# Graph network on one core: 50, 54 and 57 dense blocks in the three aggregations instead of 54 in each, seven of them built during the second and third

## The chip, the cores and the metric

One core of a Trainium2 chip, one launch. The metric is device time in microseconds (us), the median of the runs. Lower is better.

## What is computed

12,500 nodes with 128 features, and 400,000 edges sorted by their target `dst`, denser at low targets. The reference, cut:

```
h = relu(layernorm(x))
norm = deg_inv[src] * deg_inv[dst]
m = norm[:, None] * (h[src] + h[src] * h[dst] @ W1.T + b1)
x = x + leaky(segment_sum(m, dst))
h = relu(layernorm(x))
h = relu(h @ Ws0.T + (segment_sum(h[src], dst) / deg) @ Wn0.T + c0)
h =      h @ Ws1.T + (segment_sum(h[src], dst) / deg) @ Wn1.T + c1
x = x + h
```

There are three aggregations, each a segment sum of table rows over the edges of every target. The linear maps of the second and third are applied to the table before the sum.

## The kernel before, in words

The nodes are 98 tiles of 128 targets. An aggregation (`nth` = 0, 1, 2) computes each tile in one of two ways.

**Dense tiles**, the first `GROUPS` = 54 (most edges). Tile g has a count matrix ("block") of 128 targets by 12,544 sources in bf16, 3,136 KB, in one of two buffers `stage[0..1]`. The tile's sum is 98 matmuls (`product`, L1358), each with a block of 128 x 128 counts as weights and 384 columns (388 in aggregation 0) of the table `Xp`, which lies in SBUF in three bf16 parts.

**Tail tiles**, the other 44, are summed from gathered rows: one indirect DMA of 128 table rows for each 128 edges ("chunk") on GpSimd's queue (`gather`, L1187), a one-hot S on VectorE for each subgroup of up to five chunks (`ready`, L1601), and one matmul for each chunk (`subgroup`, L1296). A tail has 24 chunks at tile 54, 18 near the end and 12 in the last, 888 in all. The ring has room for five subgroups. `gather` and `ready` of a subgroup wait until the one five before has been used.

**Building a block** is done once, in aggregation 0. Edges of a node (or of two neighbours, from tile 14 on) are a "visit": a matmul (L1402) of a one-hot of the source's low 7 bits and a one-hot of its tile (128 x 196 with two nodes), into PSUM. From tile 16 on a block has 64 visits. VectorE makes one-hots for six visits at a time into one of three buffers (`one_hots`, L1573 and L1576), each buffer waiting until the visits that used it are done. ScalarE copies two visits' result out of PSUM into `stage` (`evict`, L1004); visits may be two such units ahead of it. SyncE stores the finished block to DRAM (L938). Step s of aggregation 0 runs the products of block s among the visits of block s+1, with at most one tail tile in it (44 tails over steps 2 to 53).

**Aggregations 1 and 2** build nothing. Two blocks are still in `stage`; for each step s from 2 on, SyncE loads one (`load_c`, L855: it waits for the end of step s-2). TensorE runs 98 products in each step, with the tail subgroups put among them at even distances (`due_at`). Each has 54 steps.

After its sum a tile goes through small work in a pipeline of places, two places for a step (dense, tail): `take`, `settle`, `finish`, `split_tile` on VectorE (L1648 to L1712), transposes and small fp32 matmuls on TensorE (L1308, L1316, L1324, L1334), copies on ScalarE (L1015, L1016, L1038 to L1070). In aggregation 2 only `take` is left. All queues are in program order, written out by hand.

**Ahead of aggregation 0** (0 to about 390 us) the edges are prepared: VectorE counts edges below each node, seven tiles at a time (L1473, L1474); after eight of these groups (`SPLIT_AT = 8 * HALF`, L1491) SyncE stores the first part of the edge positions and issues one small read for each of 36 batches of blocks (L841), later the second part (L844).

The order on TensorE in aggregations 1 and 2:

```
for i, (s, e) in enumerate(sequence):
    for j in drain_after[nth - 1].get(i, []): ...
    while n < n_subs and due_at[n] <= i:
        subgroup(nth, n)
        n += 1
    product(nth, s, e)
```

Of the kernel before, what the change touches and what calls it, by code (L numbers as in the profile page):

```python
# [16 lines left out]
P = 128  # L18
# [6 lines left out]
HALF = 7  # L25
# [7 lines left out]
GROUPS = 54  # L33
HEAD = GROUPS * P
TAIL_EDGE = 294400
# [32 lines left out]
def plan_batches(n_nodes, n_edges):  # L68
# [14 lines left out]
    for n in reversed(ns):  # L83
        vs = [visits_of(a, n, n_nodes, n_edges)]
        for count in ((8, 28, 32, 60) if a == 0 else (P // 2, P // 2) if vs[0] * P > 384 else (P,)):
            batches.append((a, n, [visits_of(a + i * n, n, n_nodes, n_edges) for i in range(count)]))
            a += count * n
    return batches
# [39 lines left out]
def program(nc, x, src, dst, W1, b1, Ws0, Wn0, c0, Ws1, Wn1, c1, out, n_nodes):  # L128
# [24 lines left out]
    units_of = [[q for q in range(len(units)) if unit_groups[q][0] == g] for g in range(GROUPS)]  # L153
    evicts_of = [max(evicts_to[q] - (len(unit_groups[q]) - 1 - unit_groups[q].index(g)) for q in range(len(units)) if g in unit_groups[q])
                 for g in range(GROUPS)]
    first_of = [min(q for q in range(len(units)) if g in unit_groups[q]) for g in range(GROUPS)]
# [3 lines left out]
    visits_in = [sum(unit_visits[q] for q in units_of[g]) for g in range(GROUPS)]  # L160
# [4 lines left out]
    assert hots_to[-1] == all_visits and all(r == 1 for r in rounds)  # L165

# [9 lines left out]
    n_subs = len(subs)  # L176
    gathered_to, so_far = [], [0] * RSUBS
    for u in range(3 * n_subs):
        so_far[u % RSUBS] += subs[u % n_subs][2]
        gathered_to.append(so_far[u % RSUBS])  # L180
    before_sub = [sum(n * max(1.0, 18 / tail_visits[i]) for i, _, n in subs[:u]) for u in range(n_subs)]
    due_at = [int(FIRST_DUE + (GROUPS * tiles - 8 - FIRST_DUE) * before_sub[u] / before_sub[-1]) for u in range(n_subs)]
    tail_at = [None] * GROUPS
    for i in range(tails):
        s = due_at[subs_of[i][-1]] // tiles
        assert s >= 2 and tail_at[s] is None
        tail_at[s] = i
    dense_at = [list(range(GROUPS))]
    for nth in range(1, 3):
        dense_at.append(dense_at[-1][:-3:-1] + dense_at[-1][:-2])  # L190
    places = 2 * GROUPS + EMPTY
    rank_at, order = [], []
    for nth in range(3):
        tile_at = [t for s in range(GROUPS) for t in (dense_at[nth][s], None if tail_at[s] is None else GROUPS + tail_at[s])]
# [3 lines left out]
    assert rows == tiles * P and tiles == loops * 2 * HALF and n_edges == iters * STEP and iters <= P and AT_ONCE * tiles <= BANK  # L198
# [9 lines left out]
    counts = nc.dram_tensor("counts", [GROUPS, P, tiles * P], BF16).ap()  # L208
# [6 lines left out]
    with ExitStack() as ctx:  # L215
# [85 lines left out]
        landing += [view(A_LAND, deepest[k] * P, 2) for k in range(2, n_batches)]  # L301
# [46 lines left out]
        SPLIT_AT = 8 * HALF  # L348
# [111 lines left out]
        def at(nth, p):  # L460

            return rank_at[nth][p] if 0 <= p < places else None

        def ticks_of(s):

            return range(2 * s, 2 * s + 2 if s < GROUPS - 1 else places)
# [19 lines left out]
        def during(w):  # L486

            return min(hot_at(w + 1) - 1 + HOTS, len(hots) - 1)
# [8 lines left out]
        for g in range(1, GROUPS):  # L497
            s = g - 1
            due = [] if tail_at[s] is None else subs_of[tail_at[s]]
# [5 lines left out]
            for e in range(2):  # L505
# [3 lines left out]
        last_due = [] if tail_at[GROUPS - 1] is None else subs_of[tail_at[GROUPS - 1]]  # L509
        hots_before_batch = [next(i for i in range(len(hots)) if hots[i][0] == k) for k in range(n_batches)]  # L510
        key_before = {hots_before_batch[k] + min(5, sum(f[0] == k for f in hots) - 1): k + 1 for k in range(1, n_batches - 1)}
        hot_of = [(i, e) for i, (_, m, _, _, n) in enumerate([(f[0], f[2], 0, 0, f[4]) for f in hots]) for e in range(m * n)]
        CAST, TURN_DST, GET_DST, TURN_SRC, GET_SRC = 100, 180, 230, 260, 310
        turned = (11, 11, deepest_tail - 22)
        assert GET_SRC < visits_in[0] - 20 and tails * 11 <= BANK and 0 < turned[2] <= 11
# [5 lines left out]
        sequence += [(1, e) for e in range(early // 2, tiles)] + [(s, e) for s in range(2, GROUPS) for e in range(tiles)]  # L521
        drain_after = ({10: [places], 18: [places + 1], 26: [places + 2], 50: [places + 3, places + 4, places + 5], 58: [places + 6], 66: [places + 7]},
                       {18: [places, places + 1, places + 2], 26: [places + 3], 34: [places + 4]})
        last_ticks = dict(zip((8, 28, 48, 62, 76, 82, 87, 91, 94, 96, 97), ticks_of(GROUPS - 1)))
        ready_after = [[] for _ in range(GROUPS)]
        for n in range(RSUBS, n_subs):
            ready_after[max(1, due_at[n - RSUBS] // tiles)].append(n)
        assert len(last_ticks) == EMPTY + 2 and at(1, 3) is None and at(2, 3) is None
# [284 lines left out]
        def _(sp):  # L813
# [89 lines left out]
            def load_ahead(nth, e):  # L903
# [6 lines left out]
                else:  # L910
                    sp.wait_ge(s_agg, nth * GROUPS)
# [3 lines left out]
            def last_step(nth):  # L915

                for j in ticks_of(GROUPS - 1):
                    load_next(nth, j)
# [5 lines left out]
            with sp.If(load_flag(sp, 0)):  # L924
# [7 lines left out]
                for g in range(GROUPS):  # L932
                    if g:
                        for j in ticks_of(g - 1):
# [7 lines left out]
                for nth in range(1, 3):  # L942
                    for k in range(3):
                        sp.wait_ge(s_pst[k], stored(k, nth * tiles))
                    if nth == 2:
                        for k in range(3):
                            sp.wait_ge(s_x1st[k], 16 * thirds(tiles, k))
                    load_first(nth)
                    for s in range(GROUPS - 1):
                        for j in ticks_of(s):  # L950
# [848 lines left out]
```

## Time and profile before

| | |
|---|---|
| median of 3 runs | 5116.73 us (5094.92 to 5118.95) |
| the profiled execution | 5090.41 us, span 5088.7 us |
| busy: TensorE / VectorE / ScalarE / GpSimd | 79% / 39% / 22% / 55% of the span |
| mean granted TensorE clock | 0.933 of 2.4 GHz |
| chain that ended last | TensorE 73%, of it L1358 53%, L1296 9%, L1402 7%; "issue" 11%; VectorE 7% |
| DMA | 914.9 MB, mean 180 GB/s |

Busy time of TensorE is that of modelled, overlapping matmuls, so it doesn't say how near the engine is to its limit. Starts of instructions and their distances are measured.

### The profile page before, as it was taken

To read this page: it belongs to the slowest core of one execution; us is meant where nothing else is said; L and a number is where in the kernel's file an instruction comes from. 1 tells how busy PE (TensorE), PEld (TensorE's weight loads), DVE (VectorE), ACT (ScalarE), POOL (GpSimd) and SP (SyncE) were. 2 spreads that over 40 slices of the span, in tenths; PEclk is the share of its full clock that TensorE was granted. 3 is DMA by queue.
4 is the path that set the end of the run, shared out by engine and by line. 5 is a ranking of instruction groups with operands and counts; after the bars stand their busy time and mean duration, and the time that the engine had idled before them with its cause. 6 is when DMAs were issued, how large, how long until landed. Compare 5 with 4: busy or idle time off the path is not lost.

```text
span 5088.7 us, 66517 instructions
## 1 busy us (share of the span) xinstructions
PE 3996.0 (79%) x24579; PEld 2352.5 (46%) x24579; DVE 1981.0 (39%) x5188; ACT 1129.7 (22%) x2916; POOL 2806.9 (55%) x2876
## 2 busy tenths in 40 slices
PE   0049677788788878888788888888888888888888
PEld 0035444455454545555444444544444444444444
DVE  3499566666565656565121122221211111111111
ACT  0034344455454545454000000000000000000000
POOL 5303533554645454552666666666646666666665
PEclk9999888899998999999899999999989999999999
DMA  4153334444444444456555555665665565566654
GB/s 140 36 137 125 116 129 143 144 164 165 154 161 146 167 149 164 152 169 215 203 209 209 211 211 209 218 222 205 225 224 206 208 217 212 197 226 213 212 209 170
DMA packets 384983, 914.86 MB, mean 180 GB/s; under 512 B 74278, under 2 KB 318543, under 8 KB 363929
## 3 DMA queue, kind: packets, MB, share of 16 engines
q1 hardware_dynamic: 193728, 603.15, 31.9%
q0 software_dynamic: 132960, 275.90, 18.3%
q10 hardware_dynamic: 57968, 31.48, 2.3%
q8 instruction: 202, 3.31, 0.3%
q14 instruction: 125, 1.02, 0.1%
HBM read 672.23 MB, written 238.88 MB: 179 GB/s over the span
## 4 chain that ended last, share of the span: by engine, by line
PE 73%; issue 11%; DVE 7%; another core or an unknown queue 4%; ACT 2%; DMA 2%; SPq 0%; POOL 0%; ACTq 0%; DVEq 0%; POOLq 0%
PE ps L1358 53%; PE ps L1296 9%; PE ps L1402 7%; ACT arena L1004 2%; PE ps L1324 2%; DVE arena L1573 2%; DVE arena L1576 2%; DMA arena<-in_src 1%; DMA table<-arena 1%; PE ps L1316 0%; PE ps L1308 0%; DVE stats L1479 0%; SPq L816 0%; DVE arena L1474 0%
## 5 line engine op out<-in xcount | busy, mean ns | idle before, releaser
L1187 POOL DMA_INDIRECT arena<-parts,arena x2664 | 2643.3, 992 | 1732.5 <-issue 718.1
L1358 PE MATMUL ps<-arena 128*128 128x384 bf16 (+1 forms) x15876 | 3296.7, 340 | 366.5 <-issue 321.9
L1358 PEld LDWEIGHTS ps<-arena 128*128 128x128 bf16 x15876 | 1566.2, 101 | 1458.1 <-issue 642.0
L1402 PE MATMUL ps<-arena 128*128 128x196 bf16 (+1 forms) x4910 | 1018.5, 245 | 421.1 <-issue 166.1
L1004 ACT ACTIVATE arena<-ps 128x392 bf16<-128x392 f32 x1728 | 848.5, 498 | 1088.1 <-PE ps L1402 832.1
L1601 DVE TENSOR_TENSOR arena<-arena 128x640 bf16<-128x640 bf16 (+1 forms) x582 | 268.9, 464 | 1866.5 <-remote 1485.9
L1402 PEld LDWEIGHTS ps<-arena 128*128 128x128 bf16 x4910 | 459.2, 103 | 730.6 <-issue 277.2
L1573 DVE TENSOR_TENSOR arena<-arena 128x768 bf16<-128x768 bf16 (+3 forms) x848 | 457.2, 539 | 667.0 <-PE ps L1402 513.9
L1296 PE MATMUL ps<-arena 128*128 128x384 bf16 (+1 forms) x2664 | 571.2, 340 | 53.0 <-issue 48.7
L1576 DVE TENSOR_TENSOR arena<-arena 128x1176 bf16<-128x1176 bf16 (+4 forms) x848 | 528.2, 623 | 0.0
L1296 PEld LDWEIGHTS ps<-arena 128*128 128x128 bf16 x2664 | 266.3, 101 | 270.6 <-issue 115.3
L1062 ACT ACTIVATE arena<-ps 128x128 f32<-128x128 f32 x196 | 54.3, 277 | 1018.3 <-remote 742.6
L1648 DVE TENSOR_REDUCE arena<-ps 128x128 f32<-128x384 f32 x294 | 163.0, 554 | 262.5 <-remote 177.8
L1177 POOL DMA_INDIRECT arena<-records,first_edge x36 | 48.0, 1334 | 335.6 <-PE ps L1266 321.0
L1324 PE MATMUL ps<-w_t,arena 128*128 128x256 f32 x392 | 125.0, 400 | 12.9 <-issue 7.4
L1152 POOL DMA_INDIRECT arena<-in_dst,arena x98 | 97.0, 990 | 54.8 <-issue 29.5
L1015 ACT ACTIVATE arena<-ps 128x128 bf16<-128x128 f32 x196 | 54.0, 275 | 215.9 <-remote 66.9
L1247 PE MATMUL ps<-ident,arena 128*56 128x128 f32 x1 | 0.4, 416 | 103.2 <-DVE arena L1491 103.2
L1016 ACT ACTIVATE arena<-ps 128x256 f32<-128x256 f32 x196 | 75.5, 385 | 0.1
L1324 PEld LDWEIGHTS ps<-w_t,arena 128*128 128x128 f32 x392 | 63.6, 200 | 21.7 <-issue 18.8
L1709 DVE TENSOR_TENSOR arena<-arena,bias 128x128 f32<-128x128 f32 x196 | 56.1, 286 | 28.6 <-ACT arena L1016 28.3
L1712 DVE TENSOR_TENSOR arena<-arena 128x128 bf16<-128x128 f32 x196 | 57.4, 293 | 6.7
(155 smaller groups left out, 1180.1 us busy)
## 6 DMA issues: line engine op xcount, KB each, us to landing
arena<-counts SPq DMA_DIRECT2D x104, 3136.0 KB
counts<-arena SPq DMA_DIRECT2D x54, 3136.0 KB
arena<-parts,arena POOLq DMA_INDIRECT x2664
arena<-parts SPq DMA_DIRECT2D x28, 672.0 KB, 9.6
arena<-table SPq DMA_DIRECT2D x196, 64.0 KB
parts<-arena ACTq DMA_DIRECT2D x110, 96.0 KB
parts<-arena SPq DMA_DIRECT2D x14, 679.0 KB, 6.9
parts<-arena SPq DMA_DIRECT2D x86, 96.0 KB
```

The source lines that it names most:

```text
L1004: act.activation(stage[g % 2][:, :, f - g * P:t - g * P], ps[:, q % 2, (f - a) * tiles:(t - a) * tiles].rearrange("p (n a) -> p a n", n=t ...
L1016: act.activation(yS[:, n % 3, :], bank(7, 0, 2 * P), ACT.Copy).then_inc(s_yS, 1)
L1152: pool.indirect_dma_start(near[q % 7][:, t % HALF, :], None, dst.rearrange("(c e) -> c e", e=P), bass.IndirectOffsetOnAxis(ap=near_i[:, t: ...
L1187: pool.indirect_dma_start(ring[:, m % RSUBS * CHUNKS + c, 0:W0 if nth == 0 else W1C], None, parts_of[nth], bass.IndirectOffsetOnAxis(ap=ta ...
L1296: t = pe.matmul(bank(b, 0, w), S[:, e, :], ring[:, e, 0:w], start=first + c == 0, stop=first + c == tail_visits[i] - 1, skip_group_check=True)
L1324: pe.matmul(bank(7, 0, 2 * P), hT[:, r % 2, :], w_t[:, 2 * nth + 1:2 * nth + 3, :].rearrange("p k f -> p (k f)"), start=True, stop=True).t ...
L1358: m = pe.matmul(bank(b, 0, w), stage[k][:, a, :], Xp[:, a, 0:w], start=e == 0, stop=e == tiles - 1, skip_group_check=True)
L1402: pe.matmul(bank(q % 2, b * n * tiles, (b + 1) * n * tiles), hot_low[f % HOTS][:, c * P:(c + 1) * P], hot_key[f % HOTS][:, c * n * tiles:( ...
L1573: dve.tensor_tensor(hot_low[f % HOTS][:, 0:visits * P].rearrange("p (v f e) -> p v f e", v=visits, e=2), low[:, k % 2, at_c, :].unsqueeze( ...
L1576: dve.tensor_tensor(hot_key[f % HOTS][:, 0:visits * width].rearrange("p (v f e) -> p v f e", v=visits, e=2), key[:, k % 2, at_c, :].unsque ...
L1601: dve.tensor_tensor(S[:, e:e + count, :].rearrange("p c (f e) -> p c f e", e=2), tail_rel[:, i, first:first + count, :].unsqueeze(2).to_br ...
L1648: then(dve.tensor_reduce(agg, bank(b, 0, PARTS * P).rearrange("p (k f) -> p f k", k=PARTS), AX.X, ALU.add))
```

## The change

Aggregation nth has `STEPS[nth]` dense blocks: 50, 54, 57, and 48, 44, 41 tails (984, 888, 818 chunks). Aggregation 0 builds blocks 0 to 49. In aggregation 0 every step from 2 to 49 has one tail. During steps 11, 22, 33 and 44 of aggregation 1, blocks 50 to 53 are built for the next step, and stored after it; aggregation 2 builds blocks 54 to 56 during steps 13, 27 and 41 (64 visits each, 448 in the seven). In such a step the visits stand among products 20 to 93, use PSUM banks 4 and 5, and are copied out into the buffer of step s+1, for which nothing is loaded. The one-hots come on VectorE after the step's two ticks and before `ready`; the copies on ScalarE are cut in two by the second tick. The records of these blocks are landed at the start of the aggregation (two more indirect DMAs on GpSimd's queue), turned in steps 2 and 4. `SPLIT_AT` is 9 groups, the batches are 38, and the tail edges kept start at 283,264 instead of 294,400.

```diff
-GROUPS = 54
+STEPS = (50, 54, 57)
+GROUPS = STEPS[0]
-TAIL_EDGE = 294400
+TAIL_EDGE = 283264
...
-        SPLIT_AT = 8 * HALF
+        SPLIT_AT = 9 * HALF
...
+    built_in = [{}, dict(zip((12, 23, 34, 45), range(STEPS[0], STEPS[1]))), dict(zip((14, 28, 42), range(STEPS[1], STEPS[2])))]
...
+        ends_at = {due_at[nth][subs_of[i][-1]] // tiles if nth else i + steps - tails_of[0]: i for i in range(steps - GROUPS, tails_of[0])}
...
             def load_c(nth, s):
                 k = stage_of(nth, s)
-                sp.wait_ge(s_agg, nth * GROUPS + s - 1)
+                sp.wait_ge(s_agg, steps_before[nth] + s - 1)
+                if s - 2 in built_in[nth] and nth == 1:
+                    sp.wait_ge(s_counts[k], 16 * stores_to[built_in[nth][s - 2]])
...
-                        if s + 2 < GROUPS:
+                        if s + 2 < STEPS[nth] and s + 2 not in built_in[nth]:
                             load_c(nth, s + 2)
+                        if s + 1 in built_in[nth] and nth == 1:
+                            g, k = built_in[nth][s + 1], stage_of(nth, s + 1)
+                            sp.wait_ge(s_evict, evicts_of[g])
+                            sp.dma_start(counts[g], stage[k].rearrange("p a n -> p (a n)")).then_inc(s_counts[k], 16)
...
+                        for i, j in enumerate(ticks_of(nth, s)):
+                            if nth == 1:
+                                tick(nth, j)
+                            for q in here[15 * i:15 + 17 * i]:
+                                if q == here[0]:
+                                    act.wait_ge(s_agg, steps_before[nth] + s)
+                                evict(q, k, 4)
...
+            def visit(w, bank_0):
+                q, c_0, j, v = visit_at[w]
+                width = batches[units[q][0]][1] * tiles
+                if w == visits_to[q] - unit_visits[q] and q >= 2:
+                    pe.wait_ge(s_evict, evicts_to[q - 2])
+                f, c = hot_of[w]
+                if c == 0:
+                    pe.wait_ge(s_hot, f + 1)
+                pe.matmul(bank(bank_0 + q % 2, c_0, c_0 + width), ...).then_inc(s_visit, 1)
...
                         product(nth, s, e)
+                        if s + 1 in built_in[nth]:
+                            g = built_in[nth][s + 1]
+                            if e == 20:
+                                pe.wait_ge(s_key, batches_to[nth])
+                                pe.wait_ge(s_w1free, tiles)
+                            for w in range(starts_at[g], starts_at[g + 1]):
+                                if 20 + (w - starts_at[g]) * 75 // visits_in[g] == e:
+                                    visit(w, 4)
...
+                        if s + 1 in built_in[nth]:
+                            g = built_in[nth][s + 1]
+                            for f in range(hot_at(starts_at[g]), hot_at(starts_at[g + 1])):
+                                one_hots(f)
+                        for n in ready_after[nth][s]:
                             ready(nth, n)
```

## Rows read from the trace of the kernel before

**Rows 1.** Each engine by stage; stretches cut at block stores and loads.

```profile
core 0: us, PE busy (x) PEld busy (x) DVE busy (x) ACT busy (x) POOL busy (x), PEclk, DMA share, GB/s
1075.20:2359.70 1284.50, 1053.12 (x6891) 658.89 (x6891) 780.10 (x2040) 646.52 (x1574) 663.11 (x633) 0.94 0.47 159
2359.70:2417.50 57.80, 51.11 (x295) 30.86 (x296) 27.40 (x111) 13.52 (x49) 4.08 (x5) 0.97 0.86 276
2417.50:3703.10 1285.60, 1103.01 (x6090) 616.37 (x6089) 252.48 (x719) 93.59 (x360) 839.81 (x872) 0.95 0.60 211
3791.30:5039.10 1247.80, 1066.13 (x5788) 580.09 (x5788) 195.88 (x463) 0.00 (x0) 819.91 (x851) 0.91 0.60 214
```

**Rows 2.** Waits (engine, line, releaser: us, times, longest), aggregation 2.

```profile
DVE arena L1601 <- remote: 712.5, 106, 13.8
PEld ps L1358 <- issue: 289.6, 618, 3.2
POOL arena L1187 <- issue: 232.3, 758, 0.8
POOL arena L1187 <- remote: 186.1, 83, 4.7
```

**Rows 3.** TensorE's timeline in aggregation 1, one step's part.

```profile
2928.01 3.90 PE L1358 MATMUL ps<-arena 128*128 128x384 bf16 x23
2931.75 0.81 PE L1296 MATMUL ps<-arena 128*128 128x384 bf16 x4
...
2933.86 0.27 PE L1316 MATMUL ps<-ident,arena 128*128 128x128 f32 x1
2933.97 0.60 PE L1324 MATMUL ps<-w_t,arena 128*128 128x256 f32 x2
2934.41 2.01 PE L1358 MATMUL ps<-arena 128*128 128x384 bf16 x10
...
2937.52 0.32 PE L1358 MATMUL ps<-arena 128*128 128x384 bf16 x1 [0.39 <-issue]
2938.25 0.32 PE L1358 MATMUL ps<-arena 128*128 128x384 bf16 x1 [0.41 <-issue]
```

**Rows 4.** The block stores around the four steps without a tail, SyncE's timeline.

```profile
1219.86 0.32 SPq L938 DMA_DIRECT2D counts<-arena  x1
1251.06 0.32 SPq L938 DMA_DIRECT2D counts<-arena  x1
...
1408.64 0.32 SPq L938 DMA_DIRECT2D counts<-arena  x1
1434.81 0.32 SPq L938 DMA_DIRECT2D counts<-arena  x1
...
1659.63 0.32 SPq L938 DMA_DIRECT2D counts<-arena  x1
1691.20 0.32 SPq L938 DMA_DIRECT2D counts<-arena  x1
...
1945.15 0.32 SPq L938 DMA_DIRECT2D counts<-arena  x1
1974.79 0.32 SPq L938 DMA_DIRECT2D counts<-arena  x1
```

**Rows 5.** Groups by form, 1075.2 to 2359.7: ScalarE's copies, VectorE's one-hots, GpSimd's gathers.

```profile
L1004 ACT ACTIVATE arena<-ps 128x392 bf16<-128x392 f32 x1153 | 564.7, 499 | 637.9 <-PE ps L1402 508.1 <-remote 88.6 <-issue 35.6
L1576 DVE TENSOR_TENSOR arena<-arena 128x1176 bf16<-128x1176 bf16 x377 | 288.4, 765 | 0.0
L1573 DVE TENSOR_TENSOR arena<-arena 128x768 bf16<-128x768 bf16 x376 | 208.0, 553 | 447.7 <-PE ps L1402 382.3 <-remote 60.4 <-issue 4.0
L1187 POOL DMA_INDIRECT arena<-parts,arena x617 | 647.4, 1049 | 587.8 <-PE ps L1296 405.1 <-issue 159.0 <-remote 23.7
```

**Rows 6.** Waits in the same stretch of aggregation 0.

```profile
PEld ps L1402 <- issue: 168.1, 221, 4.3
PEld ps L1402 <- ACT arena L1004: 147.6, 149, 3.4
```

**Rows 7.** Preparation: SyncE's timeline, then VectorE's.

```profile
180.32 20.79 SPq L841 DMA_DIRECT2D arena<-ends_d  x36
212.31 0.33 SPq L844 DMA_DIRECT2D ends_d<-arena  x1
...
176.26 0.22 DVE L1491 SCALAR_TENSOR_TENSOR arena<-arena 128x56 f32<-128x56 f32 x1 [9.22 <-issue]
189.59 1.09 DVE L1473 TENSOR_TENSOR arena<-arena 128x896 bf16<-128x896 int32 x1
```

**Rows 8.** VectorE's timeline in aggregation 1: first and last row around a step's two ticks.

```profile
2926.85 0.55 DVE L1648 TENSOR_REDUCE arena<-ps 128x128 f32<-128x384 f32 x1
...
2931.19 0.43 DVE L1601 TENSOR_TENSOR arena<-arena 128x512 bf16<-128x512 bf16 x1
```

More of the change, by code:

```diff
@@ L87, in plan_batches @@
             a += count * n
+    for first, last in zip(STEPS, STEPS[1:]):
+        for g in range(first, last, 2):
+            batches.append((g * P, 2, [visits_of(g * P + i * 2, 2, n_nodes, n_edges) for i in range(P if g + 1 < last else P // 2)]))
     return batches
@@ L159, in program @@
     assert all(len(unit_groups[q]) == 1 and unit_groups[q][0] < CHECKED_TO for q in checked)
-    visits_in = [sum(unit_visits[q] for q in units_of[g]) for g in range(GROUPS)]
+    visits_in = [sum(unit_visits[q] for q in units_of[g]) for g in range(STEPS[2])]
     starts_at = [int(a) for a in np.cumsum([0] + visits_in)]
@@ L165, in program @@
     assert hots_to[-1] == all_visits and all(r == 1 for r in rounds)
+    batches_to = [sum(b[0] < n * P for b in batches) for n in STEPS]
+    hots_in = [sum(batches[f[0]][0] < n * P for f in hots) for n in STEPS]
+    assert all(batches[f[0]][1] == 2 for f in hots[hots_in[0]:])
     tails = tiles - GROUPS
@@ L176, in program @@
     n_subs = len(subs)
-    gathered_to, so_far = [], [0] * RSUBS
[L178 to L192, printed above, removed]
-    for nth in range(3):
-        tile_at = [t for s in range(GROUPS) for t in (dense_at[nth][s], None if tail_at[s] is None else GROUPS + tail_at[s])]
+    tails_of = [tiles - n for n in STEPS]
+    first_sub = [subs_of[STEPS[nth] - GROUPS][0] for nth in range(3)]
+    steps_before = [sum(STEPS[:nth]) for nth in range(4)]
@@ new lines, in program @@
+    due_at, tail_at, dense_at, order, rank_at, places = [], [], [], [], [], []
+    for nth in range(3):
+        steps = STEPS[nth]
+        before_sub = [sum(n * max(1.0, 18 / tail_visits[i]) for i, _, n in subs[first_sub[nth]:u]) for u in range(n_subs)]
+        due_at.append([int(FIRST_DUE + (steps * tiles - 8 - FIRST_DUE) * before_sub[u] / before_sub[-1]) for u in range(n_subs)])
+        ends_at = {due_at[nth][subs_of[i][-1]] // tiles if nth else i + steps - tails_of[0]: i for i in range(steps - GROUPS, tails_of[0])}
+        assert len(ends_at) == tails_of[nth] and min(ends_at) >= 2
+        tail_at.append([ends_at.get(s) for s in range(steps)])
+        if nth == 0:
+            dense_at.append(list(range(steps)))
+        else:
+            kept = iter(dense_at[-1][:-3:-1] + dense_at[-1][:-2])
+            dense_at.append([built_in[nth][s] if s in built_in[nth] else next(kept) for s in range(steps)])
+        places.append(2 * steps + EMPTY)
+        tile_at = [t for s in range(steps) for t in (dense_at[nth][s], None if tail_at[nth][s] is None else GROUPS + tail_at[nth][s])]
@@ L197, in program @@
         rank_at.append([None if t is None else order[nth].index(t) for t in tile_at])
-    assert rows == tiles * P and tiles == loops * 2 * HALF and n_edges == iters * STEP and iters <= P and AT_ONCE * tiles <= BANK
+    loads_to, stores_to, so_far = {}, {}, [[0, 0], [GROUPS // 2, GROUPS // 2]]
+    for nth in range(1, 3):
+        for s in range(2, STEPS[nth]):
+            k = (s + nth) % 2
+            if s in built_in[nth]:
+                so_far[1][k] += nth == 1
+                stores_to[built_in[nth][s]] = so_far[1][k]
+            else:
+                so_far[0][k] += 1
+                loads_to[nth, s] = so_far[0][k]
     assert all(len(o) == tiles for o in order) and (n_edges - TAIL_EDGE) % P == 0
@@ L300, in program @@
         landing = [view(A_X, deepest[0] * P, 2), view(A_X + 2 * P * deepest[0], deepest[1] * P, 2)]
-        landing += [view(A_LAND, deepest[k] * P, 2) for k in range(2, n_batches)]
+        landing += [view(A_LAND + (2 * P if k > batches_to[0] and (k - batches_to[0]) % 2 else 0), deepest[k] * P, 2) for k in range(2, n_batches)]
         assert 2 * P * max(deepest[2:]) <= 1280 and 2 * P * (deepest[0] + deepest[1]) <= XP_COLS
@@ L460, in at, with ticks_of @@
         def at(nth, p):
-            return rank_at[nth][p] if 0 <= p < places else None
-        def ticks_of(s):
-            return range(2 * s, 2 * s + 2 if s < GROUPS - 1 else places)
+            return rank_at[nth][p] if 0 <= p < places[nth] else None
+        def ticks_of(nth, s):
+            return range(2 * s, 2 * s + 2 if s < STEPS[nth] - 1 else places[nth])
         def stage_of(nth, s):
@@ L498, in program @@
             s = g - 1
-            due = [] if tail_at[s] is None else subs_of[tail_at[s]]
+            due = [] if tail_at[0][s] is None else subs_of[tail_at[0][s]]
             for e, n in enumerate(due):
@@ L1729, in _ @@
                 dve.wait_ge(s_iotak, 1)
-                for f in range(len(hots)):
+                for f in range(hots_in[0]):
                     if f in key_before:
```

200 lines of the change are left out of this document (114 added, 86 removed).

## Prediction

> **What bounds the kernel now.** I read the page's chain of waits first: TensorE holds 73% of it. Then the engines by stage [rows 1], cut at the stores and loads of blocks so that each stretch is whole steps. Aggregation 0 from block 18 on is 36 steps in 1284.5 us, 35.7 each. Aggregation 1 is 51 steps in 1285.6 us, 25.2 each; aggregation 2 is 51 in 1247.8 us, 24.5 each. The reader is to see that in aggregations 1 and 2 VectorE and ScalarE are nearly empty (252 and 94 us of 1286, then 196 and none), GpSimd is busy two thirds and DMA 60%. The waits [rows 2] settle between TensorE and GpSimd: GpSimd, apart from 0.3 us ahead of each gather, stands 186 us waiting for ring room, that is for TensorE to use an old subgroup, while TensorE has no wait for a gather among its large ones, only "issue". So TensorE's stream is the bound in both, with room on GpSimd of some 15%.
>
> TensorE's stream [rows 3]: 23 products start within 3.74 us, 0.163 each, at full clock; then come stretches where one starts every 0.7 us with nothing named that it waits for. Over the whole of aggregation 2, 51 x 98 products and some 51/54 of 888 gather matmuls are 5837 in 1247.8 us, 0.214 each. The difference to 0.163 is the granted clock (0.91, so 0.179) and those stalls. So a matmul of 384 columns costs between 0.179 (if stalls are not caused by it) and 0.214 us (if they are). I take 0.214, since the stalls are spread through the whole stretch (618 of them on L1358's weight loads [rows 2]).
>
> In aggregation 0 the step holds visits too. Four steps in the stretch have no tail; the distances of the stores around them are 31.2, 26.2, 31.6 and 29.6 us [rows 4], mean 29.6. The other 32 take (1284.5 - 118.6) / 32 = 36.4. So there a tail costs 6.8 us, against 20 x 0.214 = 4.3 for its matmuls alone. Of 29.6, 98 products are 98 x 0.214 x 388/384 = 21.2 and a tile's small work about 1 (in aggregation 1 it is 0.55, from 2933.86 to 2934.41 [rows 3], and aggregation 0 has two more products). What is left, 7.4 us, is the price of a block's 64 visits, with the waits that they bring. By columns alone they are 64 x 196/384 x 0.163 = 5.3. ScalarE's copies of two visits are 0.499 us and the one-hots for six visits 0.553 + 0.765 = 1.32 [rows 5]; TensorE's waits in front of visits are half "issue", half ScalarE's copy [rows 6].
>
> A rule bears on these stalls. The Trainium skill ("Runtime: NRT & Kernel Launch", Instruction fetch mechanics) says that the sequencer fetches its instructions in 16 KiB blocks by its own DMA queue, and that this is mostly hidden. By that rule no stall belongs to an instruction as such, a visit costs its columns alone, and the sum below is 7 x 2.1 = 15 us smaller; the stalls of 0.7 us in the trace are then something else, and no row tells what.
>
> **Aggregation 0: four blocks fewer, four tails more.** Four steps go: products, visits, copies, one-hots, stores. Without their tails they are 4 x 29.6 = 118.6 us. 48 tails instead of 44, and the four new ones have 24 chunks, not 20: 4 x (6.8 + 4 x 0.214) = 30.6. Small work of 98 tiles stays. Sum **-88**. Bounds: dearest and cheapest tail-less step, and a tail at its matmuls alone (24 x 0.214 = 5.1) or at 7.7: -4 x 31.6 + 20.5 = -106, to -4 x 26.2 + 30.6 = -74. GpSimd: a gather is 1.05 us and 0.3 ahead of it [rows 5], so 24 chunks are 32 us in the early steps, and later 20 are 27, both inside a step of 36 us; it waited 405 us for ring room in this stretch, so I cost its extra 96 gathers at nothing. If that cover were gone, they would be 96 x 1.35 = 130 us.
>
> **Aggregation 1: four blocks built.** Each 7.4 us of visits. Added to that: in the step that builds, the one-hots stand behind VectorE's two ticks, which take 4.3 us [rows 8], then 1.3 for the first; TensorE reaches product 20 after some 20 x 0.163 + 0.8 of a tail's matmuls + 0.5 of small work = 4.6 us, so it waits about 1 us. The last visit is at product 93, and the next step's first product waits for its copy: 0.5 us and the way there, against four products (0.65). About 1 us more. Behind the waiting visits on TensorE stand only products of the same step; behind one-hots on VectorE stand `ready` of subgroups due more than a step later. So 4 x (7.4 + 2) = **+38**. Records turned and keys made in steps 2 and 4: two small transposes each, under 1 us together. DMA: the build takes away a load (3,136 KB) in one step and puts load and store together in the next. A step moves 25.2 us x 211 GB/s = 5.3 MB; with a store 8.5 MB; at the most that a stretch shows (276 GB/s at a share of 0.86 [rows 1], so 321 if full) that is 26.6 us, over the step's 25.2. The load stands ahead of the store on SyncE's queue, and the tile reads behind it are three places early, so I take nothing; as a bound, 3.5 us each. Bounds: visits by columns alone 4 x 5.3 = +21; with everything 4 x 13 = +52.
>
> **Aggregation 2: three more steps, 70 chunks fewer, three blocks built.** 294 x 0.214 = +62.9; -70 x 0.214 = -15.0; 3 x (7.4 + 1), since VectorE's ticks are shorter there and ScalarE is idle, +25.2. Loads are 52 as before. Sum **+73**. Bounds: matmuls at 0.179 and visits at 5.3, 52.6 - 12.5 + 16 = +56; to 62.9 - 12.5 + 3 x 10 = +80.
>
> **Preparation.** VectorE gives the first edge positions one group of seven tiles later, 189.6 instead of 176.3 us, 13.3 later [rows 7]. SyncE's small reads (36 in 20.8 us, 0.578 each) then start at 193.6 and 38 of them end at 215.6; the second store, at 212.3 now, goes behind them. **+3.3**; nothing hides it, since the last part's reads are what VectorE waits for next.
>
> **Sum.** -88 + 38 + 73 + 3 = **+26** on the profiled execution's 5090.4 us, so 5117. That execution lies 26 below the median of the runs shown (5116.7), inside their spread; on the median it is **5143 us**. In words: aggregation 0 gives back four blocks, but the kernel builds three more in all, and at its bound engine products moved from the first to the last aggregation cost the same. TensorE's columns alone: 98 products fewer (-392 + 294), 26 gather matmuls more (+96 - 70), 192 visits more.
>
> **Rivals.**
>
> *The visits cost only their columns*, since they fill the 0.7 us stalls: -88 + 21 + (48 + 16) + 3 = 0, or +11 with the waits at both ends of a build; time 5117 to 5128. For it: nearly idle VectorE and ScalarE, and no load in a building step. Against: aggregation 0, where the same mix costs 7.4.
>
> *Faster: visits and waits vanish in idle time.* If steps of aggregation 0 are set by the round trip visit, copy, next visit, the four steps are worth the bound of -106, and in aggregations 1 and 2 the same visits run in the time in which TensorE now starts nothing (about 5 us a step). Then -106 + 8 + 51 + 3 = -44, or with -88 for the steps -26: 5073 to 5091, the middle 5082. It decides from below 3 us a block, not 7.4. For it: ScalarE's copy ends 148 us of waits in front of visits [rows 6], 4 us a step. The Trainium skill ("Perfetto Trace Analysis", Identifying the Most-Contended Engine) judges TensorE's headroom by weight-load busy share; here that is 616 of 1286 us, 48%, which would leave room for them. Against: TensorE's order is written by hand, a visit waits in line, and GpSimd waits for it.
>
> *Slower by more: the building steps stall.* If the first one-hot comes after S and ticks that themselves wait, or load and store collide, 5 to 6 us for each of seven steps on top: about +61, 5178. For it: VectorE waits long in `ready` (712 us in 106 times, 6.7 each [rows 2]), and what follows it in order is late by as much. Against: those waits end with TensorE's own progress.
>
> **How the numbers follow.** The change could be told from none beyond 0.5%, 26 us, here. Forecast 0.45, visits by columns 0.20, faster rival 0.17, large stalls 0.18. The forecast's own range is 5127 to 5165, half of it beyond 26 us. With the other cases: 5095 to 5185. Faster 0.15 (most of its rival), same 0.38 (the second case and the lower half of the forecast, with the faster rival's edge), slower 0.47.
>
> **What would show it.** Block stores: the last of the 50 near 2270 to 2275 instead of 2359.7, steps with a tail still 36. Loads of aggregation 1: ordinary distances 25 us, building steps 34 to 35. Aggregation 2: ordinary 24.5 and building 33. GpSimd's wait for ring room in aggregation 0 down by half but not gone; TensorE with no waits on gathers. Wrong if aggregation 0's steps grow past 37 (gathers late), if a building step takes under 29 us, or over 38, or if the granted clock of a stage moves by more than 0.02, which is 25 us in a stage and in no term of mine.

## The result and the profile after

| | before | after |
|---|---|---|
| median | 5117.84 us (4 runs, 5094.92 to 5136.64) | 4987.82 us (4 runs, 4966.84 to 5001.77) |
| ratio | | 0.974, 95% interval 0.969 to 0.980 |
| the profiled execution | 5090.41 us, span 5088.7 | 4966.84 us, span 4965.1 |
| mean granted clock | 0.933 | 0.946 |

Faster by 2.6%, where 0.5% slower was forecast and the widest range began at 5095 us. By stage, cut at the first block store, the first load of aggregation 1 and the first of aggregation 2:

| us | preparation | aggregation 0 | aggregation 1 | aggregation 2 |
|---|---|---|---|---|
| before | 390.8 | 2026.7 | 1373.8 | 1297.3 |
| after | 395.1 | 1942.4 | 1398.1 | 1229.4 |
| difference | +4 | -84 | +24 | **-68** |
| predicted | +3 | -88 | +38 | **+73** |

All of the surprise is in aggregation 2. It does three more dense steps and builds three blocks, and takes 68 us less.

The engines by stage (the stretches of the second and third row hold nearly the whole of aggregations 1 and 2); they answer to [rows 1]:

```profile
core 0: us, PE busy (x) PEld busy (x) DVE busy (x) ACT busy (x) POOL busy (x), PEclk, DMA share, GB/s
950.00:2180.00 1230.00, 999.44 (x6538) 626.69 (x6536) 755.36 (x1990) 601.93 (x1484) 717.69 (x689) 0.94 0.50 163
2330.00:3720.00 1390.00, 1208.33 (x6798) 687.20 (x6795) 324.98 (x874) 164.74 (x522) 874.39 (x904) 0.94 0.60 209
3740.00:4960.00 1220.00, 1093.79 (x6420) 625.60 (x6417) 233.85 (x538) 47.53 (x98) 765.73 (x792) 0.97 0.61 216
```

TensorE starts 6420 matmuls in 1220 us of aggregation 2, one in 0.190 us; before it was one in 0.216 (5788 in 1247.8 us [rows 1]). The granted clock is 0.97 instead of 0.91. So the mean distance of two starts, which the prediction had taken for a price, is another one here. The waits of the changed kernel in aggregation 2, which answer to [rows 2] (L1434 is the product, L1242 the gather, L1681 `ready`):

```profile
engine line waited for: us in total, times, longest us
DVE arena L1681 <- remote: 524.2, 70, 12.4
POOL arena L1242 <- issue: 179.4, 587, 0.9
POOL arena L1242 <- remote: 144.7, 66, 2.9
PEld ps L1434 <- issue: 140.0, 263, 2.0
```

These are of 3850 to 4850. TensorE's unexplained "issue" gaps on the weight loads fall from 290 us in 618 pieces of 1248 us [rows 2] to 140 us in 263 pieces of 1000. GpSimd's waits at the head of a subgroup (L1242, "remote") stay: 145 us of 1000, where it was 186 of 1248.

The loads on SyncE's timeline around a building step of aggregation 1 and one of aggregation 2; a built block needs no load, so the distance there spans two steps (58.02 us from 2569.83, 54.66 from 3963.27):

```profile
2545.85 0.32 SPq L887 DMA_DIRECT2D arena<-counts  x1
2569.83 0.32 SPq L887 DMA_DIRECT2D arena<-counts  x1
2627.85 0.32 SPq L887 DMA_DIRECT2D arena<-counts  x1
2649.40 0.32 SPq L887 DMA_DIRECT2D arena<-counts  x1
...
3942.57 0.32 SPq L887 DMA_DIRECT2D arena<-counts  x1
3963.27 0.32 SPq L887 DMA_DIRECT2D arena<-counts  x1
4017.93 0.32 SPq L887 DMA_DIRECT2D arena<-counts  x1
4040.69 0.32 SPq L887 DMA_DIRECT2D arena<-counts  x1
```

In aggregation 1 the ordinary step is 24.4 us (median) and the four double distances are 58.0, 57.1, 62.9 and 56.7, so a built block costs some 9.9 us (58.7 - 48.8). In aggregation 2 the ordinary step is 22.1 (25.4 before), the three double ones 54.7, 52.7 and 53.6: 9.5 each.

### The profile page after: what moved, and what is told of

It reads as the page before. It is cut to its first block, busy times and chain, and to the rows that moved or that the text cites. A ratio compares the mean times of both kernels' runs of the same rounds, so it can differ in the third digit from the quotient of the medians.

```text
span 4965.1 us, 67044 instructions
## 1 busy us (share of the span) xinstructions
PE 3948.1 (80%) x24703; PEld 2352.8 (47%) x24703; DVE 2022.3 (41%) x5265; ACT 1174.3 (24%) x3014; POOL 2846.9 (57%) x2906
## 4 chain that ended last, share of the span: by engine, by line
PE 72%; issue 10%; DVE 7%; another core or an unknown queue 5%; ACT 3%; DMA 2%; SPq 0%; POOL 0%; ACTq 0%; DVEq 0%; POOLq 0%
PE ps L1434 51%; PE ps L1357 9%; PE ps L1407 8%; ACT arena L1038 2%; DVE arena L1653 2%; PE ps L1385 2%; DVE arena L1656 2%; DMA table<-arena 1%; DMA arena<-in_dst 1%; PE ps L1377 0%; PE ps L1369 0%; DVE stats L1559 0%; SPq L846 0%; DVE arena L1729 0%
## 5 line engine op out<-in xcount | busy, mean ns | idle before, releaser
L1242 POOL DMA_INDIRECT arena<-parts,arena x2690 | 2679.9, 996 | 1730.9 <-issue 716.3
L1434 PE MATMUL ps<-arena 128*128 128x384 bf16 (+1 forms) x15778 | 3245.8, 337 | 264.9 <-issue 224.6
L1434 PEld LDWEIGHTS ps<-arena 128*128 128x128 bf16 x15778 | 1550.4, 100 | 1295.5 <-issue 465.8
L1407 PE MATMUL ps<-arena 128*128 128x196 bf16 (+1 forms) x5102 | 1076.2, 246 | 462.8 <-issue 189.0
L1038 ACT ACTIVATE arena<-ps 128x392 bf16<-128x392 f32 x1824 | 892.5, 498 | 1919.1 <-PE ps L1407 1469.6
L1681 DVE TENSOR_TENSOR arena<-arena 128x640 bf16<-128x640 bf16 (+1 forms) x587 | 269.4, 463 | 1591.7 <-remote 1286.3
L1653 DVE TENSOR_TENSOR arena<-arena 128x768 bf16<-128x768 bf16 (+3 forms) x881 | 475.9, 540 | 695.9 <-PE ps L1407 598.5
L1357 PE MATMUL ps<-arena 128*128 128x384 bf16 (+1 forms) x2690 | 573.6, 341 | 30.6 <-issue 21.3
L1656 DVE TENSOR_TENSOR arena<-arena 128x1176 bf16<-128x1176 bf16 (+4 forms) x881 | 553.5, 628 | 0.0
```

The source lines that it names most:

```text
L1038: act.activation(stage[k][:, :, a - g * P:b - g * P], ps[:, bank_0 + q % 2, 0:(b - a) * tiles].rearrange("p (n a) -> p a n", n=b - a), ACT ...
L1242: pool.indirect_dma_start(ring[:, m % RSUBS * CHUNKS + c, 0:W0 if nth == 0 else W1C], None, parts_of[nth], bass.IndirectOffsetOnAxis(ap=ta ...
L1357: t = pe.matmul(bank(b, 0, w), S[:, e, :], ring[:, e, 0:w], start=first + c == 0, stop=first + c == tail_visits[subs[n][0]] - 1, skip_grou ...
L1407: pe.matmul(bank(bank_0 + q % 2, c_0, c_0 + width), hot_low[f % HOTS][:, c * P:(c + 1) * P], hot_key[f % HOTS][:, c * width:(c + 1) * widt ...
L1434: m = pe.matmul(bank(b, 0, w), stage[k][:, a, :], Xp[:, a, 0:w], start=e == 0, stop=e == tiles - 1, skip_group_check=True)
L1653: dve.tensor_tensor(hot_low[f % HOTS][:, 0:visits * P].rearrange("p (v f e) -> p v f e", v=visits, e=2), low[:, k % 2, at_c, :].unsqueeze( ...
```

## The experiments

Theories. **Price**: the prediction's, each TensorE instruction costs what the mean shows, 0.214 us for 384 columns. **Pace**: aggregations 1 and 2 last as long as the gathers need, so a dense block more is nearly free and a gather less is worth about 1.4 us. **Chance**: the granted clock of the one profile moved. The stage of aggregation 2 is quoted for every kernel, since the kernels differ there. The runs went to different chips. The kernel before takes 5,098 and 5,100 us on one of them (two batches of runs), 5,049 on another, and 4,257 (one run) and 4,259 on two more; the first two chips and that of the first pair (5,118) are "the slower chips", the last two "the faster chips". Whole times are compared only with the kernel before on the same chip.

### The kernel before again, and the change in parts

The kernel before, and three kernels made of the change by its tuple and the steps that build: s50_54_54 builds nothing in aggregation 2; s54_54_57 builds nothing in aggregation 1 and has the 44 tails of aggregation 0 as before; s50_54_60 builds six blocks in aggregation 2, for steps 9, 18, 27, 36, 45 and 53.

```diff
-STEPS = (50, 54, 57)
+STEPS = (50, 54, 54)
+STEPS = (54, 54, 57)
+STEPS = (50, 54, 60)
```

> The kernel before once more, for a second profile of its stages. Chance theory (the last aggregation lay at a low clock, 0.91, in that one profile): its 52 loads span clearly less than the 1247.8 us of before, by 40 us or more. Both other theories (a matmul has a fixed price on TensorE; gathered chunks set the pace): 1248 us within 15.

> The change without its last part: aggregation 2 with 54 blocks, 888 chunks, nothing built in it. My prediction's prices: aggregation 0 gives 85 us, aggregation 1 costs 25, aggregation 2 as before, so 5057 where before is 5117. If the gain of the last aggregation comes from its 70 chunks fewer (chunk theory), the same number, and the whole change is 70 us faster than this one. If it comes from something else in the changed code, such as freer queues, this one is at 4990 already.

> The last part alone: 54 blocks in aggregations 0 and 1, three more built in aggregation 2 and 818 chunks in it. My prediction's prices: +73 there and +3 in the preparation, about 5193 against 5117. Chunk theory (time of aggregation 2 goes with its chunks, 1.46 us each): -68 +3, about 5052.

> Sixty blocks in aggregation 2, six built there, 760 chunks or so. My prediction's prices: another 73 us on top of the change. Chunk theory: another 58 chunks less at 1.46 us, minus nothing, so 50 to 85 us faster than the change, about 4920. A third theory, that TensorE and GpSimd are near each other: TensorE takes over between 57 and 60, so within 25 us of the change or slower.

Measured on one slower chip (kernel before 5097.81, median of 13 runs):

| | us | ratio, interval | aggregation 0 | 1 | 2 | gathers in 2 |
|---|---|---|---|---|---|---|
| again_54 | 5074.27 | | 2007.8 | 1366.3 | 1304.7 | 888 |
| s50_54_54 | 5056.18 | 0.992, 0.989 to 0.995 | 1990.3 | 1396.0 | 1299.4 | 888 |
| s54_54_57 | 5020.63 | 0.985, 0.980 to 0.990 | 2051.3 | 1373.4 | 1220.0 | 818 |
| s50_54_60 | 4924.61 | 0.967, 0.962 to 0.972 | 1963.3 | 1400.4 | 1161.8 | 749 |

Chance falls: two more traces with 888 gathers have 1299 and 1305 us. The gain belongs to the third number alone: with three more blocks there and nothing else, about -80 us; with six, about -140. Each block more is some -23 to -27 us, against +24 by price. Price falls. s50_54_60 beats both kernels, by 3.3% against the kernel before.

### What paces aggregation 2: gathers, matmuls or products left out

Five edits of the kernel before, each in aggregation 2 alone. (1) x_fewgather, r_fewgather (the count that TensorE waits for is lowered with it):

```diff
-                for c in range(count):
+                for c in range(count if nth < 2 else 1):
                     pool.indirect_dma_start(ring[...], None, parts_of[nth], ...)
```

(2) x_fewmm, r_fewmm: the same edit around the matmul of `subgroup`. (3) x_fewprod, r_fewprod:

```diff
-                m = pe.matmul(bank(b, 0, w), stage[k][:, a, :], ...)
+                if nth < 2 or e % 3 != 1 or e == tiles - 1:
+                    m = pe.matmul(bank(b, 0, w), stage[k][:, a, :], ...)
```

(4) x_narrow:

```diff
-ring[:, ..., 0:W0 if nth == 0 else W1C], None, parts_of[nth]
+ring[:, ..., 0:W0 if nth == 0 else W1C if nth == 1 else P], None,
+parts_of[nth] if nth < 2 else parts_of[nth].rearrange("r (k f) -> (r k) f", f=P)
```

(5) x_smallload, and r_narrow and r_smallload, which are (4) and (5) once more:

```diff
-                sp.dma_start(stage[k]..., counts[dense_at[nth][s]])
+                cols = tiles * P if nth < 2 else 4 * P
+                sp.dma_start(stage[k]...[:, 0:cols], counts[dense_at[nth][s], :, 0:cols])
```

> The kernel before, but in aggregation 2 each gathered row has 128 columns of bf16 and not 384 (the tail tiles' sums are not the reference's; instructions and their number are unchanged). If the gathers' traffic holds up TensorE, aggregation 2 falls from 1300 us to about 1160, as with 60 blocks. If it is GpSimd's issue, or TensorE's own price, it stays at 1300 within 15.

> The kernel before, but in aggregation 2 only the first chunk of each subgroup is gathered, 194 of 888 (tail sums not the reference's); TensorE's instructions are unchanged. My prediction's price (a matmul costs 0.214 us whatever is gathered): 1300 us. If gathering sets the pace in any way, traffic or GpSimd: about 54 x 18.6 + ends = 1040 to 1080.

> The kernel before, but in aggregation 2 only one matmul for each subgroup, 694 fewer (tail sums not the reference's); all 888 gathers stay. My prediction's price: 694 x 0.214 = 149 us less, 1150. If GpSimd's 1.27 us a chunk set the pace: unchanged, 1285 to 1300. Something of both gives a fall by 694 x 0.163 = 113 at most.

> The kernel before, but in aggregation 2 each block load brings 128 KB and not 3,136 (dense sums not the reference's). If block loads cause TensorE's stalls, aggregation 2 falls by up to 240 us. If gathering does, it stays within 20 us, since the gathers are as many as before.

> The kernel before once more, for its stages on the chip that the other kernels of this call run on. Two chips have been seen so far: one on which it takes about 5,100 us (aggregation 2: 1,305 us for 888 gathers, 1.47 us each) and one on which it took 4,256.5 us once, with no profile. If the pace of GpSimd's gathers sets aggregations 1 and 2 on the faster one: both near 888 x 1.27 = 1,130 us, with TensorE's idle time put down to the gathers' transfers. If TensorE's stream sets them there: no such waits, and TensorE busy to the end of every step.

> The kernel after, on the same chip. Gather pace: aggregation 2 shorter than in r_54 in proportion to its gathers, 818 of 888, so by 8%: about -90 us on a chip where it takes 1,120, -100 where it takes 1,300; aggregation 1 (888 in both) within 30 us. TensorE's stream at a fixed price for each instruction (the prediction's): aggregation 2 longer by 3 x 98 x 0.214 + 192 visits less 70 matmuls, +73 us, on either chip. Total by gather pace: -84 (aggregation 0) + 30 - 90 to 100 = about -140; by the fixed price +26.

> Leaves out, in aggregation 2 of the kernel before, all gathers of a subgroup but its first (194 instead of 888); the matmuls stay, on old rows of the ring. Gather pace: aggregation 2 falls by over 100 us, to what TensorE's stream alone takes. On a chip where it takes 1,300: if the gathers only hold TensorE back through its 'issue' gaps, these fall from some 240 us to under 100 and the stage to 1,060 to 1,150; if the gaps are TensorE's own (one for so many instructions), the stage stays within 30 us of 1,300. On a chip where it takes 1,120: about 995, as seen once.

> Leaves out, in aggregation 2 of the kernel before, all matmuls on gathered rows but one for each subgroup (194 instead of 888); all gathers stay. Gather pace: the stage changes by under 20 us (1,126 was seen once on the faster chip). Fixed price for each matmul: 694 x 0.214 = -149 us.

> Leaves out, in aggregation 2 of the kernel before, 32 of the 98 products of each step (1,728 of 5,292); all gathers, their matmuls, one-hots and block loads stay. What TensorE must do falls from about 990 us at the full clock (6,180 matmuls of 0.16) to about 715. A pace of the gathers that belongs to GpSimd and its transfers alone: the stage stays within 30 us of the 1,290 to 1,305 seen on the slower chip (of 1,123 on the faster). GpSimd alone at its 1.27 us an issue and nothing else slower: 1,130 on both chips, which would make the 170 us above it on the slower one a coupling of TensorE's work with the gathers. TensorE's fixed price: 1,728 x 0.214 = -370 us, to about 930.

> As x_fewprod (32 of 98 products left out in aggregation 2 of the kernel before; all gathers and their matmuls stay), in the hope of the slower chip. If the gathers have a pace of 1.46 us there whatever TensorE does, the stage stays at 1,290 to 1,305 us. If TensorE's own work slows them down, it falls to 1,130, GpSimd's issue alone. On a faster chip it repeats 1,123.

The stage of aggregation 2, in us:

| | gathers | matmuls on them | products | slower chips | faster chips |
|---|---|---|---|---|---|
| kernel before | 888 | 888 | 5,292 | 1304.0 (r_54) | no profile; its aggregation 1, with 888 too: 1153 to 1159 |
| few gathers | **194** | 888 | 5,292 | **995.7** | **995.5** |
| few gather matmuls | 888 | 194 | 5,292 | 1286.1 | 1126.4 |
| few products | 888 | 888 | 3,564 | 1280.4 | 1122.9 |
| narrow rows | 888 | 888 | 5,292 | | 1120.5 |
| small block loads | 888 | 888 | 5,292 | | 1123.3 |
| the change (r_57) | 818 | 818 | 5,586, and 192 visits | 1228.2 | |

Taking 694 matmuls or 1,728 products away from TensorE gives 18 and 24 us, where price has 149 and 370; taking gathers away gives 308 us on the slower chip and some 128 on the faster. With so few gathers TensorE alone needs 996 us on either chip. r_fewprod ran on another slower chip than the rest of its column (kernel before 5048.79 there, aggregation 1 1340 us against 1367 in r_54, which bounds how much of its 24 us is the chip's). On the faster chips the stage is 1,120 to 1,126 us in all four kernels with 888 gathers: the row widths and the loads don't matter. r_narrow and r_smallload were meant for a slower chip but ran on another faster one and gave 1124.5 and 1119.7. So it isn't shown for the slower chips that the bytes of gathers and loads don't matter there.

On the faster chip TensorE stands waiting for gathered rows, as here in x_fewprod:

```profile
3618.41 1.44 PE L1296 MATMUL ps<-arena 128*128 128x384 bf16 x4 [3.58 <-DMA arena<-parts,arena]
```

GpSimd's line between the first and the last load of the stage, in x_fewprod, r_54, r_57 and r_fewprod, in this order (busy, mean of one | idle before, by releaser):

```profile
L1187 POOL DMA_INDIRECT arena<-parts,arena x861 | 820.5, 953 | 262.3 <-issue 259.0 <-PE ps L1296 3.4
```

```profile
L1187 POOL DMA_INDIRECT arena<-parts,arena x854 | 824.1, 965 | 432.3 <-issue 237.2 <-remote 180.7 <-PE ps L1296 14.4
```

```profile
L1243 POOL DMA_INDIRECT arena<-parts,arena x788 | 766.1, 972 | 419.4 <-issue 212.0 <-remote 170.3 <-PE ps L1358 37.1
```

```profile
L1187 POOL DMA_INDIRECT arena<-parts,arena x869 | 833.3, 959 | 412.6 <-issue 250.2 <-remote 147.6 <-PE ps L1296 14.8
```

The reader is to see two terms. Busy and "issue" together are one price per gather in all four: 1079.5 / 861 = 1.25, 1061.3 / 854 = 1.24, 1.24 and 1.25 us. On the faster chip that is all, the engine never stops. On the slower ones a second term stands beside it, pauses at the head of a subgroup: 195 us (r_54), 207 (r_57) and 162 (r_fewprod). They shrink little when a third of the products goes. With 190 us taken for them, a fit and no more, aggregation 2 would be gathers x 1.24 + 190: 888 x 1.24 + 190 = 1291 (1297 to 1305 measured), 818: 1204 (1220 to 1229), 749: 1119 (1162). It is 16 to 25 us short at 57 blocks and 43 at 60, as TensorE's own stream comes nearer.

TensorE's waits over the same stretches, in r_54, r_fewgather and r_fewprod:

```profile
PEld ps L1358 <- issue: 295.8, 595, 4.1
```

```profile
PEld ps L1358 <- issue: 0.7, 1, 0.7
```

```profile
PEld ps L1359 <- issue: 455.7, 864, 2.7
```

The gaps are no property of TensorE's instructions: they vanish without the gathers and grow when products are left out. Nor are they the fetching of instructions: r_fewgather moves the same 46 blocks on the DMA queue for instructions as r_54. One such stretch in r_fewprod, TensorE, then GpSimd, then VectorE:

```profile
4206.62 2.76 PE L1359 MATMUL ps<-arena 128*128 128x384 bf16 x16
4209.22 0.81 PE L1296 MATMUL ps<-arena 128*128 128x384 bf16 x4
...
4213.64 0.32 PE L1359 MATMUL ps<-arena 128*128 128x384 bf16 x1 [1.08 <-issue]
...
4215.81 0.48 PE L1359 MATMUL ps<-arena 128*128 128x384 bf16 x1 [0.79 <-issue]
4216.51 0.48 PE L1296 MATMUL ps<-arena 128*128 128x384 bf16 x1 [0.22 <-issue]
4218.60 0.48 PE L1296 MATMUL ps<-arena 128*128 128x384 bf16 x1 [1.61 <-issue]
4220.01 0.49 PE L1296 MATMUL ps<-arena 128*128 128x384 bf16 x1 [0.94 <-issue]
4221.39 0.48 PE L1296 MATMUL ps<-arena 128*128 128x384 bf16 x1 [0.89 <-issue]
4221.67 4.39 PE L1359 MATMUL ps<-arena 128*128 128x384 bf16 x15
```

```profile
4217.27 0.95 POOL L1187 DMA_INDIRECT arena<-parts,arena  x1 [0.30 <-issue]
4218.52 0.95 POOL L1187 DMA_INDIRECT arena<-parts,arena  x1 [0.30 <-issue]
4221.75 1.01 POOL L1187 DMA_INDIRECT arena<-parts,arena  x1 [2.28 <-remote]
```

```profile
4221.52 0.82 DVE L1602 TENSOR_TENSOR arena<-arena 128x512 bf16<-128x512 bf16 x2 [3.82 <-remote]
```

Matmuls trickle, one in 0.7 to 2 us, and TensorE is quick again as GpSimd resumes (4221.67, 4221.75). Counting groups of two and more starts that are over 0.6 us apart, with at most 1 us of quick starts between them, r_fewprod has 51 in 1,245 us, mean 10.4 us, of which 50 hold a pause of GpSimd of over 0.6 us; r_54 has 55 of mean 5.7 and r_57 44 of mean 3.5, and every one holds a pause. In these three the median distance from a group's end to the nearest end of a pause is 0.4 us. x_fewprod, on the faster chip, has no such group and no pause.

The pause isn't the wait for TensorE that the program's text suggests. Gather and `ready` wait on one semaphore, which the last matmul of the subgroup five before raises. Here that is the last of the four from 4209.22 on, which started at 4209.71, and both waiting engines go on 12 us later, 0.23 us apart. So it is in the others: of 91 pauses in r_54, 86 began after the needed matmul had ended (its end is modelled, its start measured), and the gather came a median 6.9 us after that end, with some 20 further matmuls started; 55 of 55 in r_fewprod, with 12.4 us. Two controls: in r_fewgather, on r_54's chip, 186 of 187 pauses end 0.27 us after the needed matmul, and on a faster chip, in s50_56_60 below, all 107 do. So on the slower chips both engines learn late that a matmul is done, at the end of a stretch in which TensorE trickles. Whether the matmul ends later than its modelled end or the signal is late, and what holds up both, isn't shown; it goes with the gathers.

r_57 repeated the result on the slower chip: 4985.23 us, ratio 0.975 (0.970 to 0.980); its stages 1957.7, 1397.8 and 1228.2 against r_54's 2008.5, 1367.1 and 1304.0.

### Does it hold in aggregation 1, and on other chips

s50_56_60 has STEPS = (50, 56, 60), six blocks built in aggregation 1 (for steps 9, 18, 27, 36, 45 and 51) and four in aggregation 2 (for 11, 22, 33 and 45). r_57b is the changed kernel again.

> 50, 56 and 60 dense blocks, six built in aggregation 1 and four in aggregation 2: 841 or so gathers in aggregation 1 in place of 888, 750 in aggregation 2 as in the variant 50, 54, 60. Gather pace: aggregation 1 about -65 us for some 45 gathers less, +15 for two more built blocks and their waits, aggregation 2 about -15 (two blocks fewer to build): 4,925 - 65 = about 4,860 on the slower chip. Fixed price for TensorE's instructions: +45 us in aggregation 1, so about 4,950.

> The kernel after, beside r_fewprod. On the slower chip again 4,985. On a faster one, where aggregation 2 of the kernel before takes 1,123 us for 888 gathers: the gathers' pace gives 818 x 1.27 = 1,039, TensorE at the full clock 0.16 x (57 x 98 + 818) + 31 for the visits = 1,056; so about 1,065, with TensorE as the bound, and the whole kernel about 4,256 - 45 (aggregation 0) + 10 - 58 = 4,165. The prediction's fixed price would give more than 4,256.

r_57b came on the chip of r_fewprod: 4936.19 against 5048.79 us, ratio 0.976 (0.972 to 0.981), aggregation 2 1208.5. The gain is the same on the slower chips (0.974, 0.975, 0.976). s50_56_60 came on a faster chip: 4172.34 against 4259.06 us, ratio 0.980 (0.978 to 0.982), so neither of its numbers could be met as written. Its stages are 1560.0, 1146.7 and 1094.8, where kernels like the one before have 1596 to 1607 and 1153 to 1159 in aggregations 0 and 1, and in aggregation 2 about 1,130 (the edited kernels' 1,120 to 1,126, whose whole times are 7 to 15 us under the kernel before). The engines from the first to the last load of its aggregation 2, and then those of x_fewprod:

```profile
3074.90:4123.10 1048.20, 1046.61 (x6535) 630.73 (x6533) 235.37 (x528) 64.05 (x130) 717.93 (x738) 1.00 0.70 250
```

```profile
3126.80:4208.50 1081.70, 799.17 (x4198) 438.51 (x4197) 194.68 (x464) 0.00 (x0) 819.64 (x861) 0.86 0.70 247
```

With 60 blocks TensorE starts 6,535 matmuls in 1,048 us, one in 0.160, at the full clock (2.4 GHz), and GpSimd waits 141 us for it: the bound has moved from GpSimd to TensorE. So past about 60 blocks no more should be had on the faster chips; none was run with more. On the slower chips s50_54_60 is half way there: only 34 of its 95 pauses began after the needed matmul had ended. In aggregation 1 six built blocks and 47 gathers less gave about -8 us there, where the expectation for a slower chip had -50; there too TensorE is the bound now, busy 99% of the time (1062.75 of 1075 us from 1975 on, at clock 1.00). On a slower chip this kernel wasn't run, nor was the changed kernel on a faster one: whether 56 pays there, and what 57 gives here, is open.

## Why the prediction was wrong

**The preparation**, +3.3: +4.3 measured; right, though traces of one kernel differ here by up to 11 us.

**Aggregation 0**, -88: -84 in the first pair. Over all traces on slower chips but the one at 5,049 us (six with 54 blocks: mean 2023; four with 50: mean 1963) it is -60, less than the smaller bound of -74, and r_57 against r_54 is -51. The sign holds, the size was half as large again as what came, and the first pair's agreement was partly luck. Part of the miss is the term for the four added tails, 30.6 us: they fall in the first 18 blocks, whose stores take 45 us more in the first pair (684.5 to 729.1) and 44 in the second (680.6 to 724.2).

**Aggregation 1**, +38: +30 (means 1398 of four and 1368 of six traces). A building step costs 9.4 predicted and 9.9 by the loads' distances; what the pairs of stages lack, the ordinary steps give back (24.4 against 25.1).

**Aggregation 2**, +73: -68 in the first pair, -76 in the second and over the means (1301 and 1226). This is the step that failed, in these words: "So TensorE's stream is the bound in both, with room on GpSimd of some 15%", and from it "294 x 0.214 = +62.9; -70 x 0.214 = -15.0". The mean distance of TensorE's starts, 0.214 us, was taken as a price; it was the quotient of a stage set by the gathers and the number of matmuls in it. The runs put in its place: products next to nothing (1,728 fewer gave 24 us at most), 70 gathers x 1.24 = -87, and the three building steps, which do cost something locally (9.5 each by the loads) but leave the ordinary steps shorter. The 11 us between -87 and -76 are not put down to anything by a run. The "room" was misread from its rows: "stands 186 us waiting for ring room, that is for TensorE to use an old subgroup" holds for few of these waits. In the trace of the kernel before, 85 of the 91 pauses began after the needed matmul had ended, and the gather followed a median 6.6 us after that end. So they say nothing of TensorE's stream as the bound; they are a part of the gathers' pace on the slower chips and no reserve.

The prediction had the hint in its own rows: stalls of 0.7 us "with nothing named that it waits for" are nearly a quarter of the stage (290 of 1248 us [rows 2]), and it priced instructions by them. Its lower bound, 0.179, still made each block a cost; a bound of nothing, by the reading that TensorE had time over, was left out. GpSimd's extra gathers of aggregation 0 were costed at nothing, and the same question wasn't asked the other way round for the gathers that go.

**The rivals.** "Faster: visits and waits vanish in idle time" had the right sign and the right place in part (TensorE's idle time), but it still charged 51 us for aggregation 2, and 5082 is 94 us above the result. The Trainium skill ("Perfetto Trace Analysis", Identifying the Most-Contended Engine), which judges by weight-load busy share, was the better guide: 48% in aggregation 1 [rows 1], and products did fit in. Between the first and last load of aggregation 2 the share is 577.85 of 1255.20 us (46%) in r_54 and 60% in s50_56_60, where TensorE is at its limit. "The visits cost only their columns" and "slower by more" fell.

**What was to show it.** Blocks' last store in aggregation 0: 2278.8, near the 2270 to 2275 named, but 2301.7 in r_57. Building steps lie in the stated 29 to 38 us (33.6 and 31.6 by the double distances). Ordinary steps of aggregation 2 were to be 24.5 and are 22.1. The clock is the sign of a wrong sum that came: it was to move by at most 0.02 and moved by 0.06 in that stage.

## What to carry to other kernels

An engine that is "busy" and has unnamed small gaps all through a stage isn't shown to be the bound: look at what each other engine spends on one of its instructions too, and see what repeats (here about 1.24 us of GpSimd for a gather, on every chip). A wait on a semaphore isn't a wait for the work that raises it unless that work ends just before: compare the two times. Where GpSimd issues a gather for each 128 rows, count gathers first; here a matmul more cost next to nothing until TensorE's starts were 0.16 us apart without gaps. Kernels that leave out work, on either side, settled this, and a change should be tested on the size beside it: of those tried on a slower chip 60 was better than 57.

## What the runs showed of the hardware that was not expected

- The same kernel takes 5,100 us on one chip and 4,257 on another. The three aggregations are 13 to 20% shorter on the latter, the preparation 7% (about 395 and 368 us); aggregation 2 without most of its gathers takes 996 us on both.
- An indirect gather of 128 rows of 768 bytes costs GpSimd 1.25 us from start to start, and with 256-byte rows the stage is the same (1120.5 against 1123).
- On the slower chips VectorE and GpSimd go on a median 2 to 12 us after the modelled end of the matmul whose semaphore they wait for, both at once; on a faster one (s50_56_60) 0.27 us after it. The stage's time doesn't tell this, only the two times side by side do.
- The granted clock was higher where TensorE had less idle time. Between the first and last load of aggregation 2, on slower chips, its mean and TensorE's busy share were 0.78 and 71% (r_fewprod), 0.86 and 81% (r_fewmm), 0.92 and 85% (r_54), 0.97 and 90% (r_57), 0.99 and 97% (s50_54_60), 1.00 and 100% (r_fewgather). Where another engine sets the stage, more matmuls came with a higher clock for each.
